# A linear-attention and mixture-of-experts layer on one core: the order of batch 3's step, and of what surrounds it

## The reference, cut to what matters

```python
x = x + attn(layernorm(x))
    # q, k, v = x @ W.T + b;  phi = elu(.) + 1
    # kv_sum = cumsum(phi_k * v, axis=1)         (along the tokens)
    # out = (phi_q * kv_sum * SCALE) @ Wo.T + bo
x = x + ffn(layernorm(x))
    # logits = x @ router_w; top 2 of 8, softmax over the two
    # routed: silu(x @ w1g[e]) * (x @ w1u[e]) @ w2[e], weighted by the score
    # shared: silu(x @ w_gate) * (x @ w_up) @ w_down   (1024 wide)
```

## Time and profile before

| what | value |
|---|---|
| median of 3 runs | 362.24 us (362.10 to 362.59) |
| profiled execution, its own time | 362.81 us |
| its span, first to last instruction | 361.2 us |
| mean granted clock of PE | 0.997 |
| PE busy | 342.9 us, 95% |
| weight loads of PE | 259.6 us, 72% |
| DVE busy | 236.0 us, 65% |
| ACT busy | 215.2 us, 60% |
| POOL busy | 198.3 us, 55% |

### The profile page before, as it was taken

The page is one execution under the profiler, slowest core; times in us unless marked ns, Lnnn a source line. Parts: engine busy times, 40 slices in busy tenths (PEclk is TensorE's granted clock), DMA queues, the critical chain, the costliest instruction groups (busy, mean ns, idle before and its releaser), DMA issues.

```text
span 361.2 us, 9304 instructions
## 1 busy us (share of the span) xinstructions
PE 342.9 (95%) x3007; PEld 259.6 (72%) x3007; DVE 236.0 (65%) x579; ACT 215.2 (60%) x389; POOL 198.3 (55%) x294
## 2 busy tenths in 40 slices
PE   7998889889999999999999999999999999999993
PEld 7877778678888888888888555556556566666662
DVE  4979984977889888787798655454544544433431
ACT  3669547878797796974545445544554555455452
POOL 4858578678474886828233842453344344444335
PEclk9999999999999999999999999999999999999998
DMA  7976171256466565554877455978486686856550
GB/s 189 385 202 162 74 138 47 86 119 187 91 181 191 119 184 111 135 163 149 238 233 182 104 67 94 102 69 114 68 115 93 89 102 79 118 91 103 87 72 10
DMA packets 77468, 46.43 MB, mean 129 GB/s; under 512 B 61040, under 2 KB 72560, under 8 KB 77040
## 3 DMA queue, kind: packets, MB, share of 16 engines
q1 hardware_dynamic: 63088, 35.08, 39.6%
q0 software_dynamic: 9664, 10.71, 19.6%
q10 hardware_dynamic: 4672, 0.07, 1.1%
HBM read 19.09 MB, written 12.97 MB: 89 GB/s over the span
## 4 chain that ended last, share of the span: by engine, by line
PE 71%; POOL 11%; DVE 7%; issue 6%; ACT 3%; DMA 1%; POOLq 0%; DVEq 0%; ACTq 0%
PE bU L1047 13%; PE bG L1047 12%; PE bD L936 7%; PE bV L1070 7%; PE bU L238 7%; PE bG L238 6%; PE bQ L1070 6%; PE bV L238 3%; POOL x_rows L571 3%; PE bK L238 3%; PE bK L1027 2%; PE bT L936 1%; PE bT L837 1%; DVE ab L1498 1%; PE bQ L238 1%
## 5 line engine op out<-in xcount | busy, mean ns | idle before, releaser
L1498 DVE SCALAR_TENSOR_TENSOR ab<-bU,sg 128x512 f32<-128x512 f32 x64 | 44.1, 690 | 69.5 <-PE bU L1047 47.5
L765 POOL DMA_INDIRECT out_y<-xs,dst_row x32 | 49.7, 1552 | 61.8 <-DMA out_y<-xs,dst_row 30.1
L1182 ACT ACTIVATE sg<-bG 128x512 f32<-128x512 f32 x64 | 38.0, 593 | 46.0 <-PE bG L1047 26.5
L571 POOL DMA_INDIRECT x_rows<-rows,slot_u x32 | 42.3, 1321 | 18.9 <-issue 9.8
L1047 PE MATMUL bG<-we,work 128*128 (+1 forms) x216 | 52.6, 380 | 0.0
L1047 PE MATMUL bU<-we,work 128*128 (+1 forms) x216 | 52.6, 379 | 0.0
L1325 ACT ACTIVATE ws_h<-ab 128x512 f16<-128x512 f32 x36 | 22.7, 630 | 41.4 <-DVE ab L1498 37.6
L1778 DVE TENSOR_TENSOR ws_h<-ab,ws_h 128x512 f16<-128x512 f32 x36 | 24.9, 693 | 20.8 <-ACT ws_h L1325 17.9
L1189 ACT ACTIVATE ah<-ab 128x512 f16<-128x512 f32 x32 | 20.1, 630 | 29.6 <-DVE ab L1498 25.6
L1047 PEld LDWEIGHTS bG<-we,work 128*128 128x128 f16 (+1 forms) x216 | 20.7, 99 | 19.5 <-issue 1.9
L1047 PEld LDWEIGHTS bU<-we,work 128*128 128x128 f16 (+1 forms) x216 | 19.8, 99 | 17.4
(11 more groups left out here) (330 smaller groups left out, 829.6 us busy)
## 6 DMA issues: line engine op xcount, KB each, us to landing
stage<-in_w_expert SPq DMA_DIRECT2D x24, 512.0 KB, 4.0
we<-in_w_shared SPq DMA_DIRECT2D x3, 1024.0 KB, 12.0
xs<-bo POOLq DMA_DIRECT2D x8, 256.0 KB, 4.4
out_y<-xs SPq DMA_DIRECT2D x8, 256.0 KB, 2.7
xs<-in_x SPq DMA_DIRECT2D x1, 1280.0 KB, 18.8
x_rows<-we SPq DMA_DIRECT2D x9, 134.0 KB
xs<-in_x SPq DMA_DIRECT2D x3, 256.0 KB, 3.6
work<-x_rows SPq DMA_TRANSPOSE x40
```

What stands on the lines that cost most here:

```text
L571: pool.indirect_dma_start(xrows, bass.IndirectOffsetOnAxis(ap=slot_u[q][:, k, t:t + 1], axis=0), rows2[q][:, t, :].bitcast(U16), None).the ...
L765: pool.indirect_dma_start(out_rows, bass.IndirectOffsetOnAxis(ap=dst_row[:, b:b + 1], axis=0), ya[b % NY], None, bounds_check=NT * P - 1, ...
L1182: act.activation(sg[q][:], src[:], ACT.Silu, scale=1.0 / WS).then_inc(S["sg_done"], 1)
L1498: dve.scalar_tensor_tensor(out=ab[q][:], in0=src[:], scalar=1.0 / WS, in1=sg[q][:], op0=ALU.mult, op1=ALU.mult).then_inc(S["a_done"], 1)
```

## The change

In batch 3's step (the first of the loop) the low half of batch 2's rows, the gated products and the silus stand ahead of the running sums and of the second norm, on DVE and ACT; PE has its k projection of batch 3 ahead of the attention output of batch 2, which moves from behind `gate_up(0, 2)` to there, and its `down(1, 0)` ahead of `route(2)`, `attend_out(3)` behind `gate_up(1, 2)`. `route(1)` and `ranks(1)` stand later, too. Two groups of matmuls on ones (20 and 16) go. On ACT the k and q exponentials of batch 3 and a load of the silu table stand ahead of `normed2(2)`. On DVE the keys, sums, queries and context of batch 2 stand behind the first three quarters of batch 0's gated products. On POOL the second norm of batch 2 is only the power, with `ON_DVE` at 3, and `add_bo(3)`, `add_bo(4)` and `slot_constants(3)` stand elsewhere. The loop's branches with i > 3 keep the order of before, and SP's program is not touched.

```diff
--- before.py
+++ after.py
@@ -266,7 +266,7 @@
             return w[:, m, :].rearrange("p (k n) -> p k n", k=KC)[:, :, cols], src.rearrange("p (k n) -> p k n", k=KC)[:, :, cols]
 
 
-        ON_DVE = 2
+        ON_DVE = 3
 
 
         def ln2_at(i):
@@ -650,21 +650,24 @@
             pow2(1)
             gaps(0)
             slot_constants(2)
+            add_taken(0)
+            slot_constants(3)
+            to_rows(0)
             add_bo(3)
-            add_taken(0)
-            to_rows(0)
-            norm2(2)
+            gaps(1)
+            pow2(2)
             token_ids(2)
-            gaps(1)
             add_taken(1)
-            slot_constants(3)
             to_rows(1)
             for i in range(3, B):
                 if i < B - 1:
                     norm1(i + 1)
+                if 3 < i < B - 1:
                     add_bo(i + 1)
                 token_ids(i)
                 gaps(i - 1)
+                if i == 3:
+                    add_bo(i + 1)
                 norm2(i)
                 add_taken(i - 1)
                 to_rows(i - 1)
@@ -894,8 +897,6 @@
                     if n in (0, 2):
                         for s, (w, lo) in enumerate(((wh, 0), (wh, 1), (wl, 0))):
                             if s == 2:
-                                if n == 2 and m == 0:
-                                    warm(16, bT)
                                 pe.wait_ge(S["sh_lo"], 3 * (n // 2) + m + 1)
                             for c in range(2):
                                 at = (2 * f + c) * P
@@ -961,26 +962,32 @@
             pe.wait_ge(S["const_pool"], 6)
             gate_up(0, 0)
             gate_up(0, 1)
-            warm(20, bD)
             ranks(0)
             down(0, 0)
             gate_up(0, 2)
-            attend_out(2)
-            route(1)
             down(0, 1)
             gate_up(0, 3)
+            route(1)
             down(0, 2)
-            ranks(1)
+            project(3, "k")
+            attend_out(2)
             for i in range(3, B):
                 j = i - 2
-                project(i, "kqv")
+                project(i, "qv" if i == 3 else "kqv")
+                if i == 3:
+                    ranks(1)
                 down(j - 1, 3)
                 gate_up(j, 0)
                 gate_up(j, 1)
+                if i == 3:
+                    down(j, 0)
                 route(i - 1)
-                attend_out(i)
-                down(j, 0)
+                if i > 3:
+                    attend_out(i)
+                    down(j, 0)
                 gate_up(j, 2)
+                if i == 3:
+                    attend_out(i)
                 ranks(i - 1)
                 down(j, 1)
                 gate_up(j, 3)
@@ -1124,6 +1131,9 @@
 
             def load_exp():
                 act.activation(spare[:], bias[:, 0, 0:1], ACT.Exp)
+
+            def load_silu():
+                act.activation(spare[:], bias[:, 0, 0:1], ACT.Silu)
 
             def context_hi(i):
                 act.wait_ge(S["cx_done"], i + 1)
@@ -1242,42 +1252,59 @@
             shared_hi(0, 1)
             exps(2, "q")
             silu(0, 0)
+            shared_hi(1, 1)
             act_hi(0, 0)
+            silu(1, 1)
             normed2(1)
+            act_hi(0, 1)
             row_hi2(1)
-            silu(1, 1)
-            act_hi(0, 1)
-            context_hi(2)
             choice(0)
-            normed1(3)
-            shared_hi(1, 1)
-            row_hi1(3)
             shared_hi(2, 1)
             silu(2, 0)
+            normed1(3)
+            row_hi1(3)
             act_hi(0, 2)
             silu(3, 1)
+            load_exp()
+            context_hi(2)
             act_hi(0, 3)
+            exps(3)
+            load_silu()
             normed2(2)
             row_hi2(2)
-            choice(1)
             for i in range(3, B):
                 j = i - 2
                 n = NP * j
                 first = 0 if i in FOUR else 1
-                exps(i)
+                if i > 3:
+                    exps(i)
                 silu(n, 0)
+                if i == 3:
+                    choice(1)
+                    act_hi(j, 0)
                 expert_hi(part_of_step(i, first))
+                if i == 3:
+                    silu(n + 1, 1)
+                    expert_hi(part_of_step(i, first + 1))
                 context_hi(i)
-                act_hi(j, 0)
-                silu(n + 1, 1)
+                if i > 3:
+                    act_hi(j, 0)
+                    silu(n + 1, 1)
                 act_hi(j, 1)
+                if i == 3:
+                    expert_hi(part_of_step(i, first + 2))
+                    silu(n + 2, 0)
                 if i < B - 1:
                     normed1(i + 1)
                     row_hi1(i + 1)
-                expert_hi(part_of_step(i, first + 1))
-                choice(i - 1)
-                expert_hi(part_of_step(i, first + 2))
-                silu(n + 2, 0)
+                if i > 3:
+                    expert_hi(part_of_step(i, first + 1))
+                if i > 3:
+                    choice(i - 1)
+                    expert_hi(part_of_step(i, first + 2))
+                    silu(n + 2, 0)
+                else:
+                    choice(i - 1)
                 act_hi(j, 2)
                 silu(n + 3, 1)
                 if i < B - 1:
@@ -1617,70 +1644,96 @@
             residual(1)
             stats2(1)
             moments2(1)
-            keys(2)
+            logits(0, 0)
+            logits(0, 1)
+            logits(0, 2)
             swiglu(0, 0)
+            shared_lo(2, 0)
             for k in range(4):
                 newton2(1, k)
-            logits(0, 0)
-            logits(0, 1)
-            sums(2)
             act_lo(0, 0)
-            logits(0, 2)
-            shared_lo(2, 0)
-            queries(2)
             swiglu(1, 1)
-            context(2)
+            shared_lo(0, 1)
+            shared_lo(1, 1)
+            act_lo(0, 1)
             row_lo(1, 1)
-            act_lo(0, 1)
             slots(0, 0)
             slots(0, 1)
-            shared_lo(0, 1)
+            swiglu(2, 0)
+            row_lo(0, 3)
+            keys(2)
+            shared_lo(2, 1)
+            act_lo(0, 2)
+            sums(2)
+            queries(2)
+            context(2)
+            swiglu(3, 1)
+            logits(1, 0)
             context_lo(2)
-            shared_lo(1, 1)
-            row_lo(0, 3)
-            swiglu(2, 0)
+            logits(1, 1)
+            logits(1, 2)
             residual(2)
             stats2(2)
             moments2(2)
-            act_lo(0, 2)
-            logits(1, 0)
-            logits(1, 1)
-            shared_lo(2, 1)
-            swiglu(3, 1)
-            logits(1, 2)
             act_lo(0, 3)
-            row_lo(1, 2)
+            for k in range(4):
+                newton2(2, k)
             slots(1, 0)
             slots(1, 1)
             for i in range(3, B):
                 j = i - 2
                 n, ahead = NP * j, i < B - 1
-                if ahead:
+                if i == 3:
+                    keys(i)
+                    row_lo(1, i - 1)
+                    swiglu(n, 0)
+                    sums(i)
+                    shared_out(j - 1)
+                    act_lo(j, 0)
+                    queries(i)
+                    swiglu(n + 1, 1)
+                    context(i)
                     stats1(i + 1)
-                keys(i)
-                sums(i)
-                queries(i)
-                context(i)
-                swiglu(n, 0)
-                shared_out(j - 1)
-                context_lo(i)
-                act_lo(j, 0)
-                swiglu(n + 1, 1)
+                    context_lo(i)
+                else:
+                    if ahead:
+                        stats1(i + 1)
+                    keys(i)
+                    sums(i)
+                    queries(i)
+                    context(i)
+                    swiglu(n, 0)
+                    shared_out(j - 1)
+                    context_lo(i)
+                    act_lo(j, 0)
+                if i > 3:
+                    swiglu(n + 1, 1)
                 logits(i - 1, 0)
                 logits(i - 1, 1)
+                if i == 3:
+                    logits(i - 1, 2)
+                    act_lo(j, 1)
                 residual(i)
-                logits(i - 1, 2)
+                if i == 3:
+                    swiglu(n + 2, 0)
+                else:
+                    logits(i - 1, 2)
                 stats2(i)
                 moments2(i)
-                act_lo(j, 1)
+                if i > 3:
+                    act_lo(j, 1)
                 if ahead:
                     row_lo(0, i + 1)
                 first = 0 if i in FOUR else 1
+                if i == 3:
+                    act_lo(j, 2)
                 expert_lo(part_of_step(i, first))
-                swiglu(n + 2, 0)
+                if i > 3:
+                    swiglu(n + 2, 0)
                 expert_lo(part_of_step(i, first + 1))
```

(3 more changed lines are left out.)

## The result

The changed kernel takes 360.57 us (median of five runs, 359.44 to 360.73) against 362.24 before: a ratio of 0.9947 with a 95% interval of 0.9931 to 0.9963, faster by 1.7 us. Forecast were 357.7 and a gain of 4.5. The profiled execution is the fastest of the five, 359.44 us with a span of 357.7; against the profiled one of before (362.81, span 361.2) that is 3.4 to 3.5 us. So there are two shortfalls to find: one in the trace, and one between this execution and the other four.

What follows compares the result with a forecast made beforehand. PE was taken to set the pace late in the kernel: 4.1 us from batch 4's earlier start plus 0.4 made 4.5, so 362.81 became 358.3, and the median, 0.57 lower, 357.7 us; range 355.8 to 360.6.

Steps and rivals of the forecast that it cites:

- What bounds the kernel: PE sets the pace late in the kernel, so any earlier start there moves the end by the same amount.
- Front part: Batches 0 to 2: DVE's context(2) ends at 51.4, 8 us later, covered by PE's unbroken batch 0 groups; warm-ups cost nothing.
- Scatters and norm: POOL: batch 1's four scatters end at 67.1 (6.6 with wake-up), then batch 4's norm takes 3.1, ending at 70.2.
- Batch 4's rows to PE: Norm at 70.2, DVE's low half at 72.8, transposes on SP: batch 4's projections start at 76.7 instead of 80.84, 4.1 won.
- The term of 3.95: Time from the end of DVE's low half to PE's first product, through two transposes on SP: 3.95 us.
- Batch 4 and 5's steps: After batch 4's start: its step loses 0.4 us of waiting for a gated product; batch 5's counted only in a rival.
- The clock: Fourth rival: pause before batch 4's projections drops PE to 1.2 GHz, costing 4 to 5 us: 362.2, no difference; chance 0.05.
- The pause forecast: PE waits 2.8 us ahead of batch 4's projections at 76.7, where the longest pause shown was 1.64.
- From the trace to the median: Median taken 0.57 us under the profiled execution, as in the kernel before: 358.3 becomes 357.7.
- given back in part: Second rival: norm 4.2, scatters a microsecond longer, projections at 78.8, the 0.4 not had: 2.0 won, 360.2; chance 0.17.
- slower: Third rival: context(2) past 55.5 delays everything behind it, projections(4) start past 80.84: 1.3 slower, 363.5; chance 0.10.
- ring: Attention output(2) through exponentials, norm, tanh(1), scatters(1), norm(4) to transposes, over four engines; 4.1 in hand, 5.4 late if slow.

Runs made afterwards that it cites:

- the repeated run: The changed kernel, unaltered, run once more beside later experiments: 360.06 us, ratio 0.9930 to the kernel before; its profiled execution took 360.55.
- the earlier choice: Changed kernel with batch 1's choice between batch 3's k and q exponentials, its slots before the Newton steps: 359.59 us; with batch 4's bo load moved too, 357.44 us.
- step alone, statistics first: Kernel before with only the new order inside batch 3's step, and batch 4's statistics back at the head of DVE's step: 366.00 us, ratio 1.0091.
- the step alone: Kernel before with only the new order inside batch 3's step, front part and both groups on ones as before: 366.64 us, ratio 1.0128.

## Why the prediction was wrong, point by point

- **What bounds the kernel** held: an earlier start of batch 4 was carried to the end, 2.83 at 78 us and 3.41 from batch 6 on.
- **Front part**: context(2) ended at 51.40, the forecast of 51.4; attention output at 52.12, forecast 52.05. The tanh pair ended at 60.55, forecast 60.4. The added table load lies where it was put, and cost next to nothing: the norm behind it started at 57.94, and what it needs from DVE was ready at 57.80.
- **Scatters and norm**: the end of the norm is 70.75, forecast 70.2. The norm itself took 3.0 (67.74 to 70.75, forecast 3.1); the excess is in the scatters, 7.15 us from tanh to last scatter where I had 6.6, and 0.15 in the tanh. The Trainium skill's rule on the port pair (SBUF — State Buffer, "Who interferes with whom"), which argued for 4.2, does not show in this norm: the row of the same place was the better guide.
- **Two steps failed.** The first, seen in the trace, is "Batch 4's rows to PE" together with its neighbour: "add_bo(3) moves behind four scatters and add_bo(4) behind the token iota and the gap; each transfer is asked for over 4 us later, at the residual". For batch 4 that is not so: bo was asked for at 72.47, where it was 72.34 before, and I did not ask what it meets. It was issued 0.82 us ahead of the transposes, on which the whole chain then waits. The term of 3.95 was taken from batch 0, where bo lies 3.36 us ahead and the pair takes 2.61; it measured 4.75, and moving that one load gives 3.80.
- These give the trace: 0.55 and 0.80, less 0.1 in between, are the 1.3 by which the start came after 76.7. Batch 4 and 5's steps gave 0.58 where I counted 0.4.
- **The clock** is the second step that failed, and the larger one for the median: the sum held nothing for it. It was a rival with a chance of 0.05, and a mean clock at the lower value is what most runs show. The pause forecast, 2.8, measured 3.03, but by luck: PE was free at 74.98 where I had 73.9, and the rows came 1.3 late. The remark that no row showed a pause as long was right; the chance did not follow from that remark. Its price was wrong the other way: not three or four groups at twice 1.31 lost in full, but 1.3 to 1.5 us, since the clock was back after some 3 us in which PE did half of its work. The Trainium skill (TensorE: Matmul & The Clock Gate, "What's actually happening") has the clock fall after an idle spell and return with activity; the trace of the repeated run agrees, 0.50 from 78 to 81 and 1.00 by 82.
- **From the trace to the median**: I had put the median 0.57 under the profiled execution, as before; it was 1.13 above. That is 1.7 of the 2.9 missing. The clock's 1.3 to 1.5 would be most of it; the median run (mean clock 0.994) was not profiled, so that its dip lies at this place is taken from the repeated run. The remaining 0.2 to 0.4 is within the spread of runs. The other 1.1 is in the trace (1.3 less 0.2 from the later steps).
- The number of the rival *given back in part*, 360.2, came close to 360.57 for other reasons than its own: no long norm, scatters half a microsecond longer instead of one, and a fall of the clock that it did not count. That is luck.
- The rival *slower* did not come. Its ring has little slack all the same: with the front part left out the new order of the step costs 3.5 to 4.4 us.

## What to carry to other kernels

When a change takes away the waits ahead of a chain, look at where that chain already ends in the trace of before: here the transposes of batch 4 came only 0.45 us earlier, and that bounded the gain. A load has to be placed by what it meets, and not only by when its data are needed: look for the transfer that the critical chain issues within the next microseconds, and put the load behind that. When a change trades several short PE waits for one long pause in front of a stretch where PE sets the pace, count a fall of the clock as a term of its own, and look at the granted clock of every run, for one profile may show either case. And try the halves of a reordering by themselves: here one alone gave nothing and the other lost 4 us, so the gain needs both.

## What the runs showed of the hardware

In the same program the clock fell after a pause of 2.97 us in one execution and stayed at 1.00 after 3.03 in another, so it is a matter of the execution and not of the program alone. In other kernels here it fell shortly after waits of 1.84 and 2.12. At the lower level a pair of 128x256 products takes 0.63 us where it takes 0.38. The transposes of SP's queue and the load of bo on POOL's share the DMA engines, and the transposes pay: 2.50 became 3.39, and 2.51 became 3.34 in the pair of runs with the earlier choice. The distance alone does not give the price: with the load 1.40 us ahead they took 2.88 (kernel before), with it 3.53 ahead 3.41 (step alone, statistics first). And 36 products on ones in a pause, which cost 0.06 us each, were followed twice by a start 1.6 to 1.8 us late; a kernel without them, the step alone, was as late.
